# Query and key rows of a relative-position attention loaded once per run of equal parts

## What is computed

```python
xn = layernorm(x)
q, k, v = heads(xn @ Wq + bq), heads(xn @ Wk + bk), heads(xn @ Wv + bv)
pos_emb = dist_emb[l - r + M - 1]                    # (512, 512, 16)
scores = q @ k.T + einsum("bhld,lrd->bhlr", q, pos_emb) + einsum("bhrd,lrd->bhlr", k, pos_emb)
probs = softmax(scores / sqrt(16))
s = layernorm(merge(probs @ v) @ Wo + bo + xn)
h = silu(einsum("td,edf->tef", n, w1) + b1)          # experts, top 2 of 8 rows combined
g = silu(x_mixed + combine(einsum("tef,efd->ted", h, w2) + b2))
out = x + s * g
```

## Time and profile before

| | us |
|---|---|
| median of three runs | 2211.05 |
| profiled execution, its own time | 2215.61 |
| span of its instructions | 2213.7 |
| PE busy | 1652.7 (75%) |
| DVE busy | 1144.9 (52%) |
| ACT busy | 1020.5 (46%) |
| POOL busy | 664.0 (30%) |

### The profile page before, as it was taken

The page is one execution under the profiler, slowest core; times in us unless marked ns, Lnnn a source line. Parts: engine busy times, 40 slices in busy tenths (PEclk is TensorE's granted clock), DMA queues, the critical chain, the costliest instruction groups (busy, mean ns, idle before and its releaser), DMA issues. The chain is left out here.

```text
span 2213.7 us, 32508 instructions
## 1 busy us (share of the span) xinstructions
PE 1652.7 (75%) x11192; PEld 1210.2 (55%) x11192; DVE 1144.9 (52%) x2980; ACT 1020.5 (46%) x2057; POOL 664.0 (30%) x711
## 2 busy tenths in 40 slices
PE   5536353027889788987989798976898998899881
PEld 2213133026777677876777687863555555555550
DVE  5722636503333244443323344435888888888870
ACT  3534110012434233333433234326878878888870
POOL 2560025821111111111111111105206446437435
PEclk9767575568999899999999899987999999999995
DMA  4445474778899999998999999969989899899851
GB/s 158 128 138 154 139 248 119 209 193 252 289 302 316 313 330 309 321 303 281 308 283 314 334 322 308 312 231 332 304 262 303 278 324 314 264 327 315 277 173 38
DMA packets 247731, 576.91 MB, mean 261 GB/s; under 512 B 40016, under 2 KB 86608, under 8 KB 246160
## 3 DMA queue, kind: packets, MB, share of 16 engines
q1 hardware_dynamic: 204160, 426.81, 58.0%
q0 software_dynamic: 43408, 148.04, 21.3%
HBM read 371.27 MB, written 203.42 MB: 260 GB/s over the span
## 5 line engine op out<-in xcount | busy, mean ns | idle before, releaser
L953 DVE TENSOR_TENSOR rel_out<-rl,rel_tile 128x1024 f32<-128x1024 f32 x256 | 307.5, 1221 | 240.7 <-PE rl L1005 169.9
L1220 ACT ACTIVATE scores<-scores,row_least 128x512 f32<-128x512 f32 x512 | 365.6, 717 | 25.1 <-DVE row_least L1253 24.5
L1253 DVE CUSTOM_DVE_ANT_1 scores<-sc,rq 128x512 f32<-128x512 f32 x512 | 336.7, 687 | 36.5 <-issue 35.2
L930 ACT COPY rel_tile<-rl 128x1024 f32<-128x1024 f32 x256 | 249.5, 1017 | 228.6 <-PE rl L1005 195.6
L1354 PE MATMUL pt<-ident,scores 128*128 128x128 f32 x2048 | 328.6, 285 | 30.8 <-DVE probsT L1259 15.9
L1026 PE MATMUL up<-rowsT,w 128*128 128x256 f32 x1280 | 326.5, 400 | 3.5 <-DMA w<-in_w 3.5
L1039 PE MATMUL dn<-w,hid 128*128 128x256 f32 x1280 | 326.2, 400 | 0.0
L938 ACT ACTIVATE hid<-up,b 128x256 f32<-128x256 f32 x320 | 134.1, 470 | 390.9 <-PE up L1026 390.2
L1354 PEld LDWEIGHTS pt<-ident,scores 128*128 128x128 f32 x2048 | 256.3, 147 | 105.6 <-DVE probsT L1259 52.9
L1026 PEld LDWEIGHTS up<-rowsT,w 128*128 128x128 f32 x1280 | 241.0, 199 | 32.1 <-issue 3.9
L1039 PEld LDWEIGHTS dn<-w,hid 128*128 128x128 f32 x1280 | 241.8, 199 | 28.4
(11 more groups left out here) (182 smaller groups left out, 1735.7 us busy)
## 6 DMA issues: line engine op xcount, KB each, us to landing
scratch_rel<-rel_out SPq DMA_DIRECT2D x256, 512.0 KB, 8.6
rq<-scratch_rel SPq DMA_DIRECT2D x256, 512.0 KB, 5.9
w<-in_w POOLq DMA_DIRECT2D x80, 1024.0 KB, 11.0
krows_sb<-scratch_stack SPq DMA_DIRECT2D x768, 64.0 KB, 5.3
scratch_parts<-part SPq DMA_DIRECT2D x96, 128.0 KB
by_head<-scratch_parts SPq DMA_DIRECT2D x16, 768.0 KB, 5.8
scratch_stack<-by_row SPq DMA_DIRECT2D x4, 3072.0 KB, 22.9
qrows_sb<-scratch_stack SPq DMA_DIRECT2D x192, 64.0 KB, 8.6
```

Of the source, the lines that this page charges most:

```text
L930: nc.scalar.copy(both[:, :, u * UN:(u + 1) * UN], rl[r][:].rearrange("p a (b l) -> p l (a b)", l=TILE)).then_inc(s_kc, 1)
L953: nc.vector.tensor_tensor(out[n % SRING][:], rl[r][:].rearrange("p a (b s) -> p (a b) s", s=TILE), both[:, u * UN:(u + 1) * UN], ALU.add). ...
L1220: nc.scalar.activation(sm[j][:, i], sm[j][:, i], ACT.Exp, bias=least[:, j, i:i + 1], scale=-1.0, accum_out=es[:, g // 2 % 2, i, 2 * j + g ...
L1253: nc.vector.tensor_tensor_reduce(sm[j][:, i].rearrange("p (c s) -> p c s", c=LT), sc[i % 2][:].rearrange("p (c s) -> p c s", c=LT), rq[j][ ...
```

## The change

The six DMAs into a 96-partition tile of equal runs become three, one for each part that occurs: 48 partitions of part 0, 32 of part 1, 16 of part 2. The HBM side of such a load is the part's 16 dimensions, put under a new leading dimension of n = 3, 2 or 1 with step 0 (`unsqueeze(0).to_broadcast`). The HBM side names the same 96 rows in the same order as before. The key tile in the attention stage (parts 0, 1, 2 / 0, 1 / 0) is cut into the same three runs, but each run there consists of different parts which follow each other in `scratch_parts`, so its HBM side is `(q d)`, 48, 32 and 16 rows with one step, and has no broadcast. The semaphore counts follow: three DMAs where six were.

```diff
+RUNS = [(0, 0, 3), (48, 1, 2), (80, 2, 1)]
...
             def load_k(x):
                 after(sp, s_kp, (x - KRING + 1) * PER_PIECE)
                 tile, p = x // PIECES, x % PIECES
-                for i, pair in enumerate(PAIRS):
-                    src = t["stack"][tile % LT, PARTS + pair[0], :, p * PIECE:(p + 1) * PIECE]
-                    sp.dma_start(kst[x % KRING][i * D:(i + 1) * D], src).then_inc(s_kl[x % KRING], 16)
+                for first, part, n in RUNS:
+                    src = t["stack"][tile % LT, PARTS + part, :, p * PIECE:(p + 1) * PIECE]
+                    dst = kst[x % KRING][first:first + n * D]
+                    sp.dma_start(dst, src.unsqueeze(0).to_broadcast([n, D, PIECE, BH])).then_inc(s_kl[x % KRING], 16)
 
             def load_q(lt, p):
-                for i, pair in enumerate(PAIRS):
-                    src = t["stack"][lt, pair[0], :, p * PIECE:(p + 1) * PIECE]
-                    sp.dma_start(qst[i * D:(i + 1) * D, p], src).then_inc(s_ql[p], 16)
+                for first, part, n in RUNS:
+                    src = t["stack"][lt, part, :, p * PIECE:(p + 1) * PIECE]
+                    dst = qst[first:first + n * D, p]
+                    sp.dma_start(dst, src.unsqueeze(0).to_broadcast([n, D, PIECE, BH])).then_inc(s_ql[p], 16)
...
-                            pe.wait_ge(s_kl[x % KRING], (x // KRING + 1) * 16 * len(PAIRS))
+                            pe.wait_ge(s_kl[x % KRING], (x // KRING + 1) * 16 * len(RUNS))
...
-                            pe.wait_ge(s_ql[u // PER_PIECE], (lt + 1) * 16 * len(PAIRS))
+                            pe.wait_ge(s_ql[u // PER_PIECE], (lt + 1) * 16 * len(RUNS))
...
-                for dst, side in ((qs, 0), (ks, 1)):
-                    for n, pair in enumerate(PAIRS):
-                        src = t["parts"][side * PARTS + pair[side], :, g * HG:(g + 1) * HG]
-                        sp.dma_start(dst[i][n * D:(n + 1) * D], src).then_inc(s_qk[i], 16)
+                for first, part, n in RUNS:
+                    src = t["parts"][part, :, g * HG:(g + 1) * HG]
+                    dst = qs[i][first:first + n * D]
+                    sp.dma_start(dst, src.unsqueeze(0).to_broadcast([n, D, HG, S])).then_inc(s_qk[i], 16)
+                    src = t["parts"][PARTS:PARTS + n, :, g * HG:(g + 1) * HG].rearrange("q d h s -> (q d) h s")
+                    sp.dma_start(ks[i][first:first + n * D], src).then_inc(s_qk[i], 16)
...
-                    pe.wait_ge(s_qk[g % 2], (g // 2 + 1) * 16 * 2 * len(PAIRS))
+                    pe.wait_ge(s_qk[g % 2], (g // 2 + 1) * 16 * 2 * len(RUNS))
```

## The result

The changed kernel takes 2808.92 us (median of four runs, 2805.4 to 2812.05) beside 2210.03 us for the kernel before: a ratio of 1.2709, with a 95% interval of 1.2678 to 1.274. The forecast was 2900 us in a range of 2650 to 3150.

What follows compares the result with a forecast made beforehand. Expert stage was taken as compute with DMA supply barely keeping up, then bound by the two busiest DMA engines. 2215.6 + 611 (expert) + 77 (attention) = 2904, less the profiled execution's offset, about 2900 us; range 2650 to 3150.

Steps and rivals of the forecast that it cites:

- The number of engines: Broadcast loads of 48 and 32 partitions get 3 and 2 engines, the last 16, limited by outermost HBM entries.
- the share of 0.54: DMA share while twelve scratch_parts stores drained before the change; read as consecutive transfers going to the same eight engines.
- The expert stage: 160 sets each add 4.4 us to the busiest engine's 895 us; stage 983 to 1594 us, +611, ends +479 and +799.
- the rival with the cheaper prices: Expert stage: few engines, but removed rows freed 0.317 us each and 0.91 contains overlap; +478, total 2690 us; chance 0.12.
- the 895 us of before: Expert stage before the change: the busiest engine's work, taken as 0.91 x 983 us.
- The attention stage: Engine needs 22.2 us per 19.8 us group, 2.4 more over 32 groups: +77 us, ends nothing and 126.
- The slack of 1.6 us a group: Attention: an engine works 18.2 of a group's 19.8 us; at the lower end this slack helps absorb the added load.
- SP's issues, semaphores, waits: 480 fewer issues in expert stage, 192 in attention, fewer semaphore packets, two edited TensorE waits: all costed at nothing.
- What would show it: Signs: small packets about 24080, expert stage near 1594 us, share 0.56, 186 GB/s, key-load share 2/16 to 3/16, clock below 0.92.
- All 16 engines: Rival: broadcast spreads over 48 partitions, key sets 46% shorter, 48 us off TensorE's key waits; about 2163 us; chance 0.11.
- Changing groups of engines: Rival: few engines per load but varying, averaging 6 rows per engine; 2205 to 2230 us; chance 0.03.
- dear variant of few engines: Rival: rows cost 0.198 us or more and the two engines idle 5%; expert +893, attention +126, 3230 us; chance 0.12.

Runs made afterwards that it cites:

- stepped kernel: Changed kernel's loads in the expert stage only, the outermost 3 or 2 entries running over position tiles instead of step 0, against the kernel before: 2721.84 us, ratio 1.2289.
- dimension-outermost: Changed kernel's three loads reordered so the HBM side has the 16 dimensions outermost and copies behind them, tables and mask permuted: 2199.73 us, ratio 0.995 to before.
- single-broadcast runs: Expert stage only, against the kernel before: just part 0 merged (broadcast of 3), 2433.16 us; just part 1 merged (broadcast of 2), 2472.01 us.

## Why the prediction was right, and what was off

**The number of engines.** Right. The forecast rested on twelve stores whose 112 small packets meant 8 engines each, and it carried this over to a source, to a load and to a step of 0. The packet counts of six kernels bear it out, and the stepped and dimension-outermost kernels separate it from the broadcast. The Trainium skill's "DMA: Bandwidth & Descriptors" says under "Rules for kernel authors" that an outermost dimension of fewer than 16 entries, for example a leading zero-stride broadcast of c copies, confines the DMA to at most c engines. The 24081 small packets agree, and so do the 28016 of the stepped kernel, whose step is not zero. That both loads land on the same engines was read from the share of 0.54; the two or three rows in flight show it for the changed kernel, and the two doses adding up agrees. Which engines these are by number no run shows.

**The expert stage.** The term was +611 us and measured +504, so it is the mis-sized one; the rival with the cheaper prices had +478 for this stage and came nearer. Here is queue 1 of the changed kernel in its expert stage:

```profile
q1 hardware_dynamic: 53018, 187.92, 32.7%
```

It held 0.327 x 1486.6 x 16 = 7778 us of engine time for 45.9 thousand rows of 4 KB, 0.1695 us a row, where the prediction took 0.176. Put into the sum, that is 160 x 33 x 0.0065 = 34 us of the 107 missing. It is a mean of which two thirds are rows of stores, though; in the stretch of key loads above, a row took 0.177 us, so this part is not sure either. The other 73 would need the six removed rows to have cost 0.32 us each instead of 0.24, the end that the earlier trace rows gave for key loads by themselves. But the mean of queue 1 in the kernel before is only 0.188 us (below), and with it the sum gives 895 + 160 x (33 x 0.1695 - 6 x 0.188) = 1609 us for an engine that had 1486.6. So the step that does not hold as it stands is to take the work of one engine, both queues' shares added and no idle time, as the length of the stage. The single-broadcast runs say the same with 0.103 to 0.114 us for a row. Whether the 895 us of before contain overlap of the two queues, as the rival had it, or the removed rows were dear, stays open.

The sum also had all weights and all stores wait for the slowest engine. For the stores that holds (13.7 us from issue to landing at most before, 23.2 after). The 1 MB weight loads took 11.0 us in the median before and 10.8 after, and TensorE's waits for weights hardly changed (69.3 and 71.4 us for `b`, 3.5 and 5.5 for `w`). The keys and the stores carried the added time.

**The attention stage.** The term was +77 us and measured +86; a group took (2698.2 - 1998.9) / 31 = 22.6 us where 22.2 were forecast. The slack of 1.6 us a group did not make the load free, so the nothing at the lower end was not met.

**SP's issues, semaphores, waits.** Costed at nothing. The kernel with the dimensions outermost removes the same issues and keeps all engines; it took 9 us less than the kernel before it was run with, so everything else in the change is worth about 10 us in the other direction.

**What would show it.** The stage was to last 1594 us and lasted 1486.6. Its share was to be 0.56 and was 0.57; the rate 186 and was 198 GB/s, in line with the shorter stage; the small packets 24080 and were 24081; the granted clock below 0.92 and was 0.80. The stretch of key loads was to lie near 2/16 to 3/16; queue 1 lay at 18.0% from 536 to 560 us, or 2.9 engines, which is what 96 rows over 33 on the busiest engines make.

**The rivals.** All 16 engines: no. Its price is now known from the kernel that has them, 2199.73 us, where I had worked out 2163. I took 46% off TensorE's waits for keys, and those hardly moved: 104.4 us before, 104.0 with the dimensions outermost. Larger loads were not the cure for these waits, and the rows' price did not fall either (0.553 x 970.2 x 16 us over 45.7 thousand rows is 0.188 us, and the kernel before gives 0.188). Changing groups of engines: no, by the rows in flight and the doses. The cheap and the dear variant of few engines, 2690 and 3230, lie on either side. The median of 2808.92 is 91 us below the forecast and 119 us above the cheap variant, about as near to the one as to the other.

Queue 1 in the expert stage of the kernel with the dimensions outermost and, below it, of the kernel before, for these two prices:

```profile
q1 hardware_dynamic: 57055, 187.26, 55.3%
```

```profile
q1 hardware_dynamic: 64792, 187.81, 54.9%
```

## What to carry to other kernels

Before merging small transfers, write down the outermost dimension of each side: a copy put in front with `unsqueeze(0)` handed the whole load to as many engines as there are copies, and the same copy one dimension further in cost nothing. A mean DMA share of 0.57 can hide two engines that set the pace; the count of small packets over the count of DMAs tells how many engines each one had. Do not count on free DMA time at a mean share of 0.9: here, at the smallest dose tried, 13 rows a set more on the busiest engines, the stage already paid in proportion. And issuing key loads behind the stores, to spare the stores, made every kernel slower.

## What had not been expected of the hardware

- Extra rows on the busiest engines cost 0.103 to 0.114 us of stage time each, about in proportion from 13 to 27 extra rows a set, though a row takes 0.17 us on its engine and the share was only 0.91.
- The 1 MB weight loads took no longer to land (11.0 us in the median, then 10.8), while a quarter of the 512 KB stores of SP's queue took over 15.7 us and none had taken over 13.7.
- The same transfers in another order, three key sets behind the stores instead of ahead of them, made the kernels 53 to 110 us slower, though VectorE's waits for stores had been the reason for the move.
